# Attention and expert kernel: the start of batch 0, with the output weights centred on GpSimd, group 1 normalised before the first squares, and two tiles projected before the bias is added

## What is computed

```python
xn = layernorm(layernorm(x), ln_gamma, ln_beta)
q, k, v = heads(xn @ w_q.T), heads(xn @ w_k.T), heads(xn @ w_v.T)   # 4 heads of 64
qn = rmsnorm(q, q_gamma) * 64 ** -0.5
kn = rmsnorm(k, k_gamma)
attn = softmax(qn @ kn.T)
x = x + layernorm((attn @ v) @ w_o.T + b_o)
chosen = argmax(layernorm(x) @ gate_w.T)                  # one of 8 experts a token
x = x + layernorm(layernorm(x) + expert_w[chosen] @ layernorm(x))
```

## Time and profile before

| | us |
|---|---|
| time, median of 3 runs (lowest, highest) | 702.9 (702.89, 704.34) |
| span of the profiled execution, first to last instruction | 689.7 |
| busy in the span: TensorE, VectorE, ScalarE, GpSimd | 609.0, 581.5, 535.0, 260.3 |
| projection phase of batch 0, first projection to first exponential | 16.2 to 89.5 |

### The profile page before, as it was taken

The page is one execution under the profiler, slowest core; times in us unless marked ns, Lnnn a source line. Parts: engine busy times, 40 slices in busy tenths (PEclk is TensorE's granted clock), DMA queues, the critical chain, the costliest instruction groups (busy, mean ns, idle before and its releaser), DMA issues.

```text
span 689.7 us, 21574 instructions
## 1 busy us (share of the span) xinstructions
PE 609.0 (88%) x8717; PEld 428.7 (62%) x8717; DVE 581.5 (84%) x1153; ACT 535.0 (78%) x870; POOL 260.3 (38%) x425
## 2 busy tenths in 40 slices
PE   4789979999999999977889889999999999657991
PEld 2577635666666666864567446666666668546880
DVE  4899968988988899898999778788878788997792
ACT  3389878989888988876588878888888888645771
POOL 3134443343333334000477533232323231066575
PEclk9699989999999999999999899999999999999996
DMA  5942168999898989412022589898989896026521
GB/s 165 294 101 57 34 122 161 164 172 177 152 179 166 177 153 184 112 62 61 24 70 62 124 161 168 152 167 151 168 153 167 151 169 158 30 94 205 184 88 49
DMA packets 60665, 92.88 MB, mean 135 GB/s; under 512 B 7057, under 2 KB 29844, under 8 KB 60566
## 3 DMA queue, kind: packets, MB, share of 16 engines
q0 software_dynamic: 35088, 66.13, 50.0%
q1 hardware_dynamic: 24902, 25.37, 12.7%
q10 hardware_dynamic: 576, 0.00, 0.0%
HBM read 15.87 MB, written 14.66 MB: 44 GB/s over the span
## 4 chain that ended last, share of the span: by engine, by line
PE 55%; DVE 24%; ACT 8%; issue 6%; DMA 4%; POOL 1%; SPq 0%; POOLq 0%; ACTq 0%; DVEq 0%
PE banks L1525 21%; PE banks L1568 8%; PE banks L1567 8%; PE banks L1569 7%; PE banks L1345 6%; DVE e_l L1103 3%; DVE x_all L1176 2%; ACT e_f L666 2%; PE banks L1397 2%; DVE st L1189 2%; DMA e_h<-e_f 2%; DVE e_l L963 1%; DMA e_x<-x_all 1%; PE banks L1422 1%; ACT x_all L666 1%
## 5 line engine op out<-in xcount | busy, mean ns | idle before, releaser
L666 ACT ACTIVATE e_f<-banks,nbias,c_ 128x1024 f32<-128x1024 f32 x172 | 200.7, 1202 | 43.0 <-PE banks L1525 31.4
L1525 PE MATMUL banks<-q_T,k_T 128*128 128x512 f16 (+1 forms) x1024 | 217.5, 385 | 8.6 <-DVE e_l L963 3.9
L1569 PE MATMUL banks<-v_mm,e_l 128*128 128x65 f16 x2048 | 203.5, 192 | 0.0
L1569 PEld LDWEIGHTS banks<-v_mm,e_l 128*128 128x128 f16 x2048 | 187.9, 98 | 0.0
L1103 DVE TENSOR_TENSOR e_l<-e_f,e_h 128x1024 f16<-128x1024 f32 x100 | 121.1, 1232 | 22.0 <-DMA e_h<-e_f 16.2
L1567 PE MATMUL banks<-v_mm,e_h 128*128 128x65 f16 x1184 | 118.9, 193 | 1.4 <-DVE e_l L1103 0.8
L1568 PE MATMUL banks<-v_mm,e_h 128*128 128x64 f16 x1184 | 119.1, 194 | 0.0
L1567 PEld LDWEIGHTS banks<-v_mm,e_h 128*128 128x128 f16 x1184 | 108.9, 97 | 13.6 <-DVE e_l L1103 2.3
L1568 PEld LDWEIGHTS banks<-v_mm,e_h 128*128 128x128 f16 x1184 | 108.5, 97 | 9.8
L1525 PEld LDWEIGHTS banks<-q_T,k_T 128*128 128x128 f16 (+1 forms) x1024 | 51.6, 96 | 99.1 <-issue 62.5
L666 ACT ACTIVATE x_all<-banks,nbias,c_ 128x1024 f32<-128x1024 f32 x84 | 98.8, 1201 | 6.6 <-DVE e_l L1103 5.5
(11 more groups left out here) (302 smaller groups left out, 1263.3 us busy)
## 6 DMA issues: line engine op xcount, KB each, us to landing
e_h<-e_f POOLq DMA_DIRECT2D x86, 256.0 KB, 3.9
e_x<-e_f POOLq DMA_DIRECT2D x62, 256.0 KB, 3.8
e_h<-x_all POOLq DMA_DIRECT2D x42, 256.0 KB, 4.2
e_x<-x_all POOLq DMA_DIRECT2D x30, 256.0 KB, 4.5
x_all<-x SPq DMA_DIRECT2D x12, 512.0 KB, 4.2
rows_d<-e_x SPq DMA_DIRECT2D x1, 5180.0 KB, 24.3
k_T<-k_T SPq DMA_DIRECT2D x16, 256.0 KB, 3.6
k_T<-rows_d SPq DMA_DIRECT2D x15, 259.0 KB, 5.5
```

The lines of the kernel that those rows point to most:

```text
L666: act.activation(whole[s % ALL % NEF], ps_S[s % ALL % 3], ACT.Exp, bias=bias_of(h, k // NT), scale=CESC).then_inc(s_E, 1)
L1525: return pe.matmul(ps_S[s % ALL % 3][:, c * BANK:(c + 1) * BANK], k_T[rows, 1 - c if cross else c, h * N + j * P:h * N + (j + 1) * P], q_T ...
L1569: ins = pe.matmul(o, low[s % ALL % NLO][:, at], v[:, 0:DH + 1], start=False, stop=j == NT - 1, skip_group_check=True)
```

## The change

Four things move, all of them ahead of tile 3 of batch 0; the arithmetic stays the same but for the forms in which it is written.

1. The output weights and bias are centred by GpSimd (a new `centre_output_weights` there: five `tensor_scalar`). The sums that it needs are made by ScalarE, as three copies that also accumulate a row sum (`output_weight_sums`). VectorE makes `CV` and `CIV` ahead of the rest (`value_constants`), since the centring needs `CIV`.
2. Group 1's statistics, root, factors and normalisation stand ahead of `squares(0)`; on VectorE the statistics stand even ahead of the bias rows, and the factors stand between them.
3. TensorE projects tile 0 whole and the queries and keys of tile 1 before it waits for the bias rows (`project_first_two`). Group 1 is transposed after tile 0's output weights.
4. `gate_of_output` stands ahead of tile 2's projection on TensorE (it stood behind tile 1's). For tiles 0 and 1 `normal_qk` stands ahead of group 2's statistics.

```diff
 # GpSimd, ahead of its first wait for s_const
+            def centre_output_weights():
+                pool.wait_ge(s_cv, 3)
+                pool.wait_ge(s_woc, KH)
+                pool.tensor_scalar(wosum[:, :], wosum[:, :], CIV, -1.0 / D, ALU.mult, ALU.mult).then_inc(s_woc, 1)
+                pool.wait_ge(s_woc, KH + 1)
+                for k in range(KH):
+                    pool.tensor_scalar(raw_wo[:, k, :], raw_wo[:, k, :], CIV, wosum[:, k:k + 1], ALU.mult, ALU.add).then_inc(s_woc, 1)
...
 # ScalarE
+            def output_weight_sums():
                 act.wait_ge(s_prep, 6)
                 act.activation(tmp[7], tmp[6], ACT.Sqrt).then_inc(s_prepA, 1)
+                act.wait_ge(s_wo, 16)
+                for k in range(KH):
+                    act.activation(sq[1][:, k * D:(k + 1) * D], raw_wo[:, k, :], ACT.Copy, accum_out=wosum[:, k:k + 1]).then_inc(s_woc, 1)
+                act.activation(sq[0][0:3, 0:D], bo_row[:, :], ACT.Copy, accum_out=bsum[:, :]).then_inc(s_bc, 1)
...
                     high_y(0)
+                    output_weight_sums()
                     prepare_bias()
-                    act.wait_ge(s_const, 1)
+                    root(1)
+                    group_normal(1, 1, 0)
+                    group_normal(1, 1, 1)
                 groups(a_act)
...
 # VectorE
                     low_y(0)
-                if b == 0:
-                    prepare_bias()
-                    constants()
-                    centre_output_weights()
+                    value_constants()
+                    whole_group_stats(1, 1)
+                    prepare_bias_rest()
+                    normal_factors(1)
+                    prepare_bias_rows()
+                    query_constants()
                     dve.wait_ge(s_ones, 2 + 2 * H + 1)
                 groups(a_dve)
...
                         sums(n, at, t)
-                        if first and t == 0:
+                        if first and t == 0 and b:
                             normal_factors(g + 1)
+                        if n < 2:
+                            normal_qk(n, t)
                         if t < 2 and gi + 2 < NG:
                             group_stats(g + 2, gi + 2, t)
                         if t == 1 and gi + 2 < NG:
                             group_aggregates(g + 2)
-                        normal_qk(n, t)
+                        if n >= 2:
+                            normal_qk(n, t)
...
 # TensorE
+            def project_first_two():
+                project_qk(0, 0)
+                project_v(0, 0)
+                project_qk(1, 1)
+                pe.wait_ge(s_b2, 3)
+                bias_qk(0)
+                bias_v(0)
+                bias_qk(1)
+                project_v(1, 1)
+                bias_v(1)
...
                         if t < TG - 1 or not last:
                             if t == TG - 1:
                                 pe.wait_ge(s_ys, g + 2)
-                            project(n + 1, t + 1)
+                            if n:
+                                project(n + 1, t + 1)
                         if n == 0:
+                            group_T(1)
                             gate_of_output()
-                        if t == 1 and not last:
+                        if t == 1 and not last and n != 1:
                             group_T(g + 1)
```

More of the change, by code:

```diff
@@ L638, in a_act @@
                             move_q(n - 2, at - 2)
-                        if t == 0 and not last:
+                        if t == 0 and not last and n:
                             if first:
@@ L1393, in project, with bias_qk, project_v, bias_v @@
                     pe.wait_ge(s_vl, n - 1)
-                y = y_both[n // TG % 2]
-                terms = three(t % TG, wqkv_h, wqkv_l, 0, 2 * D, *y)
-                for i, (l, r) in enumerate(terms):
+                for i, (l, r) in enumerate(three(t % TG, wqkv_h, wqkv_l, 0, 2 * D, *y_both[n // TG % 2])):
                     pe.matmul(ps_QK[t % 2], l, r, start=i == 0, stop=False)
-                if n == 0:
-                    pe.wait_ge(s_b2, 3)
+            def bias_qk(t):
                 pe.matmul(ps_QK[t % 2], ones3[:, :], bq3[:, 0:2 * D], start=False, stop=True)
+            def project_v(n, t):
                 if n // NT * NT > 0:
                     pe.wait_ge(s_gs, n // NT * NT)
-                products(ps_VG[t % 2], three(t % TG, wqkv_h, wqkv_l, 2 * D, 3 * D + NE, *y) + [(ones3[:, :], bq3[:, 2 * D:])]).then_inc(s_P, 1)
+                for i, (l, r) in enumerate(three(t % TG, wqkv_h, wqkv_l, 2 * D, 3 * D + NE, *y_both[n // TG % 2])):
+                    pe.matmul(ps_VG[t % 2], l, r, start=i == 0, stop=False)
+            def bias_v(t):
+                pe.matmul(ps_VG[t % 2], ones3[:, :], bq3[:, 2 * D:], start=False, stop=True).then_inc(s_P, 1)
+            def project(n, t):
+                project_qk(n, t)
+                bias_qk(t)
+                project_v(n, t)
+                bias_v(t)
+            def project_first_two():
[8 more added lines that the diff above has]
+                bias_v(1)
             def transpose_qk(n, t):
@@ L1505, in _ @@
                     pe.wait_ge(s_gs, b * NT - 2)
-                project(b * NT, 0)
+                if b:
+                    project(b * NT, 0)
+                else:
+                    project_first_two()
                 for p, (pb, ga, gb) in enumerate(PASSES):
```

62 lines of the change are left out of this document (31 added, 31 removed).

## The result

The changed kernel took 695.9 us (median of 6 runs, 693.93 to 696.73), the kernel before beside it 702.8 us (698.85 to 704.34). The ratio is 0.9891, with a 95% interval from 0.987 to 0.9913: 6.1 to 9.1 us less. In two later comparisons the unchanged pair gave 0.9927 (0.9904 to 0.9951) and 0.9917 (0.9888 to 0.9946). The mean of the three is 0.991, or 6.2 us. (The ratios are the record's and not quotients of medians; these are 0.9902, 0.9915 and 0.9941, so a few tenths of a percent are open in each.) Forecast were 6.4 us and 696.5 us.

A forecast was written before the change was run, and what follows sets the result against it. VectorE's timeline was taken to bound the stretch before `low_qk(0)`, with TensorE and ScalarE beside it. Moving that start from 36.22 to about 29.85 us gave 702.9 - 6.4 = 696.5 us, range 695.2 to 699.3.

The forecast's parts named there:

- The mark: Start of `low_qk(0)` on VectorE, at 36.22 us before; forecast at 29.5 to 29.85, 6.4 us sooner taken.
- rival 2: GpSimd's centring holds up VectorE on their shared port ahead of the bias rows: 0.7 to 1.3 us back, 697.5; chance 0.08.
- Rival 1: TensorE's clock falls again around tile 2's wait for `low_qk(0)`, slowing tiles 3 and 4: 697.2 to 700.4 us; chance 0.27.
- two-tile case: Two tiles' projections and transposes on TensorE run at the low clock, costing 3.0 to 3.9 us.
- Rivals 3 and 4: 3: an unmoving transfer bounds attention's start, 702.9, chance 0.04; 4: low clock stays on, five tiles 707, chance 0.03.
- Rival 5: The low-clock stretch around 90 to 95 us shortens, or squares come sooner: 1 us more gain, 695.3; chance 0.08.

The follow-up runs named there:

- e11: The changed kernel, unaltered, run again on the same chip as the kernel before; 701.58 us, ratio 0.9917 to the kernel before.
- e7: The changed kernel, unaltered, compared again with the kernel before; 697.95 us against 703.93, ratio 0.9927.
- e1: The changed kernel with the centring back on VectorE, behind the constants; 686.74 us, ratio 0.9944 to the kernel before.
- e4: The changed kernel with group 1's statistics, root, factors and normalisation back where they were; 690.81 us, ratio 0.9991 to the kernel before.
- e3: The changed kernel with TensorE waiting for the bias rows inside tile 0, as before; 687.21 us, ratio 0.9938 to the kernel before.
- e2: The kernel before with only centring on GpSimd, its sums on ScalarE, and CV and CIV ahead of the bias rows; 689.93 us, ratio 0.9977.
- e10: The kernel before, unchanged, against itself, on the chip of the changed kernel's last rerun; 704.3 us against 705.77, ratio 0.998.
- e0: The kernel before, unchanged, against itself, run for its profile; 691.33 us against 691.36, ratio 1.0001.

## Why the prediction was right, and where it was not

**The mark and its way there.** Right, to 0.1 us in the gain: forecast 6.4, measured 6.34 (6.35 in e11, 6.11 in e7). The first exponential started at 83.79 us, 0.64 of it from the later first projection; forecast was 83.1. By its steps: centring sums on ScalarE hidden (they end at 14.9, the bias copy waits until 16.9 for TensorE); statistics from 15.3 in VectorE's wait for the bias copy; TensorE's wait for the bias ahead of the row at 20.68, 0.49 us (forecast 0.5); GpSimd's two passes 1.09 us together, 0.55 each and under the lower bound of 0.65, done at 17.0 where TensorE wants them at 22.1. The first sums came 5.35 us behind the first projection, forecast 5.7: the forecast had the bias rows start 0.22 us later than before, which the slow bias product hid in this trace and e7 showed (0.26).

**What was missed there.** The port was weighed at the wrong place. GpSimd's new instructions met nothing; its old subtraction, unmoved in the lists, came to lie against `normal_qk(1)` and cost 1.0 us. That is rival 2's price, 0.7 to 1.3 us, by another instruction than it named. Luck made it good: the first sums were 0.36 us early, and from the last step of `normal_qk(1)` to the mark it took 3.1 us and not 3.6, since one step of VectorE's gate part had taken 0.95 us before (beside a product of GpSimd's at 34.45, where the changed kernel has none) and took 0.47 now. So the agreement to 0.1 us is the sum of three errors of 0.4 to 1.0 us that cancel, and is partly luck.

**The shares.** The text named parts and left them unadded. Undone one at a time they are worth 2.4 us (e1, centring), 3.7 (e4, group 1) and 0.8 (e3, TensorE's order) at the mark; together 6.9, for 6.34 with all. The three don't simply add up: the stall of 1.0 us is absent in e3 and e4 (0.17 us in both), so it comes only with parts 2 and 3 together, and undoing either one takes it away as well. Part 4 (`normal_qk` ahead of group 2's statistics) was not undone by itself, and its share is unknown.

**Rival 1** came true in one of three traces, at its place, with one tile at the low clock and 1.1 us, priced at 0.7 to 1.6. Its two-tile case was not seen; the dearest fall, 2.6 us in e4, followed a wait of 5.68 us. Its reading that 2.03 us of idleness preceded the fall at 21.0 is right for that trace, but such a wait does not bring the fall: in e2 (2.03 us) and e3 (2.19 us) the clock came through it at 1.00 and fell more than eight microseconds later.

**Rivals 3 and 4** are out: the gain reached the first table load whole (51.87 us against 51.88). **Rival 5**'s 1 us from the attention is not seen: between the table loads the two kernels' traces overlap.

**The step that failed** is the low end of the range: "The range goes from rival 5's 695.2". It was taken from one rival and put the scatter of the comparison itself at nothing, though the prediction says in the same place that a measurement can tell about 1.4 us. It is not even rival 5's sum: 702.9 - 6.4 - 1 gives 695.5, the rival says 695.3, the range 695.2. What the runs showed in its place: the ratio 0.9891, taken on 702.79, gives 695.1 us and a gain of 7.7, just below the range (the median, 695.9, lies in it), while the traces show 6.34 us at the mark and nothing more on the way to the first table load. Three comparisons of the same pair lie 0.36% apart, 2.5 us, and the kernel before differs from itself by 0.2% in e10. The two later ratios would have lain in the range. So the mechanism was right, and the range left out a scatter larger than the 1.3 us from the forecast to its low end. What the 1.3 us above 6.34 are in the first comparison is open, since no trace of before is on record from the chip of its times.

**A premise that was wrong**: "The median of the runs is 702.9 us, so 13.2 us lie outside it". 1.8 us lie outside the span; the other 11.4 agree with the longer last part of another chip. It did not move the forecast, since the sum was made as a difference.

## What to carry to other kernels

Take one instruction behind the changed stretch as a mark and count it from one ahead of it: here the mark moved by 6.34 us where the total time of one comparison could say only 6 to 9. Work that moves from one engine to another also moves everything behind it against everything else; look for what the old instructions will lie beside, not only the new ones. And where a change makes an engine early, ask what it does with the wait: here TensorE's wait for `low_qk(0)` was the place where 1.1 us were lost in one trace of three, and neither trace with idle matmuls in it lost them.

## What was unexpected of the hardware

- Chips differ by over 12 us in this kernel (691.4, 703.9 and 705.8 us for before). The spans of e0 and e10 lie 13.4 us apart, 13.2 of it in the last part; that is 107 to 110 us on some chips and 118 to 124 on others. The cause is open.
- The clock's fall differs from execution to execution: the changed kernel, behind the same wait of 3.2 us, kept 1.00 twice and fell to 0.50 once.
- In three traces of before the clock was low for 6.8 (e0), 13.6 (the first) and 17.1 us (e10); the longest stretch cost 0.6 us behind `low_qk(0)` (52.48 for 51.88), and none cost anything ahead of it (20.03 in all).
- The product for the bias rows, the last work ahead of the first projection, took 3.37 us in the first trace of before and 4.39 in that of the changed kernel. The first projection started between 15.9 and 17.5 us over all the traces, with no order by kernel: 15.9 in e7 and 17.5 in e11, which are one kernel.
